# Expert tiles computed in pairs with turned operands, the state-space start spread over two tiles, and a 32-row expansion

## The reference

```python
x = x + xattn(layernorm(x), ctx, mask)      # 16 heads, softmax over 257 keys
x = x + ssm(layernorm(x))
x = x + ffn(layernorm(x))

def ssm(x):                                  # state-space part
    conv = causal_conv4(x @ W_in[:, :768])   # C, B, x for 16 heads
    dt = softplus(x @ W_in[:, 768:] + dt_bias); A = A_param * dt
    norm = exp(cumsum(A)) * cumsum(exp(-cumsum(A)))
    Y = ssd(xh, A, Bh, Ch)
    return (Y[0] / norm) @ W_out.T           # Y of batch 0 only, norm of every batch

def ffn(x):                                  # 8 experts, inner width 704
    gates = softmax of the 2 largest of x @ w_router.T
    for e in range(8):
        h = silu(x @ w_gate[e]) * (x @ w_up[e])
        out += gates[:, e:e+1] * (h @ w_down[e])
```

## Time and profile before

| | us |
|---|---|
| median of 3 runs (1501.18 to 1503.05) | 1502.03 |
| the profiled execution, its own time | 1488.71 |
| its span, first to last instruction | 1486.7 |
| TensorE busy in the span | 1410.8 (95%) |
| VectorE busy | 1124.9 (76%) |
| ScalarE busy | 996.1 (67%) |
| GpSimd busy | 833.8 (56%) |
| mean granted TensorE clock | 0.966 |

### The profile page before, as it was taken

The page is one execution under the profiler, slowest core; times in us unless marked ns, Lnnn a source line. Parts: engine busy times, 40 slices in busy tenths (PEclk is TensorE's granted clock), DMA queues, the critical chain, the costliest instruction groups (busy, mean ns, idle before and its releaser), DMA issues.

```text
span 1486.7 us, 53570 instructions
## 1 busy us (share of the span) xinstructions
PE 1410.8 (95%) x15668; PEld 1288.0 (87%) x15669; DVE 1124.9 (76%) x3999; ACT 996.1 (67%) x2482; POOL 833.8 (56%) x1401
## 2 busy tenths in 40 slices
PE   6969999999999999999999998579999999999997
PEld 5858888888888888888888887379999999999997
DVE  3647888888888888888888886468878777787775
ACT  4726777777777777777777775067777776777674
POOL 3514665665666656656656553236666665565554
PEclk9969999999999999999999998589999999999999
DMA  6212464454433433433433321435655555555554
GB/s 189 67 30 73 120 200 136 144 192 131 122 98 96 127 93 99 122 101 90 126 96 106 86 70 55 159 120 149 162 141 151 158 142 145 144 163 142 141 147 111
DMA packets 102009, 183.80 MB, mean 124 GB/s; under 512 B 19393, under 2 KB 61377, under 8 KB 101793
## 3 DMA queue, kind: packets, MB, share of 16 engines
q1 hardware_dynamic: 86272, 164.35, 36.5%
q0 software_dynamic: 15680, 18.76, 7.1%
HBM read 152.63 MB, written 31.13 MB: 124 GB/s over the span
## 4 chain that ended last, share of the span: by engine, by line
PE 84%; DMA 2%; issue 2%; POOL 2%; DVE 1%; ACT 1%; POOLq 1%; DVEq 0%; ACTq 0%; SPq 0%
PE k L412 16%; PE m L412 12%; PE v_p L412 11%; PE y_p L1478 9%; PE up_p L1478 9%; PE gate_p L1478 8%; PE sc L412 5%; PE pt L476 5%; PE v_p L476 4%; PE ht_p L1517 3%; PE m L496 2%; DMA par<-zbuf,gi 2%; PE z_p L1484 1%; POOL gi L1668 1%; POOLq L1667 0%
## 5 line engine op out<-in xcount | busy, mean ns | idle before, releaser
L738 ACT ACTIVATE wd<-wd,nmx 128x257 f32<-128x257 f32 x512 | 255.7, 503 | 31.0 <-DVE nmx L884 26.7
L714 ACT ACTIVATE wd<-v_p 128x512 f32<-128x512 f32 x256 | 152.6, 596 | 163.8 <-PE k L412 136.5
L1305 POOL TENSOR_TENSOR ctx_lo<-wd,ctx_hi 128x516 fp32r<-128x516 f32 x128 | 167.0, 1304 | 130.5 <-ACT ctx_hi L714 130.5
L884 DVE CUSTOM_DVE_ANT_0 wd<-sc,wd 128x257 f32<-128x257 f32 x512 | 191.4, 421 | 63.6 <-PE sc L412 57.3
L1680 POOL DMA_INDIRECT out<-par,oi x71 | 113.5, 1599 | 146.5 <-ACT par L1586 145.9
L412 PE MATMUL k<-ctx_hi,wkh 128*128 128x256 f32 x512 | 159.3, 311 | 1.7 <-POOL ctx_lo L1305 1.4
L1557 ACT ACTIVATE uw_hi<-wu 128x1408 fp32r x71 | 98.3, 1385 | 85.1 <-PE up_p L1478 84.8
L1668 POOL COPY oi<-par 128x4 int32 x71 | 148.1, 2087 | 0.0
L1615 DVE TENSOR_TENSOR uw_lo<-wu,uw_hi 128x1408 fp32r<-128x1408 f32 x71 | 115.4, 1625 | 41.3 <-ACT uw_hi L1557 41.3
L412 PE MATMUL k<-ctx_lo,wkh 128*128 128x256 f32 x512 | 145.3, 284 | 0.0
L1615 DVE TENSOR_TENSOR gw_lo<-wg,gw_hi 128x1408 fp32r<-128x1408 f32 x71 | 115.4, 1625 | 39.2 <-ACT gw_hi L1557 39.2
(11 more groups left out here) (200 smaller groups left out, 4678.8 us busy)
## 6 DMA issues: line engine op xcount, KB each, us to landing
dl<-d_low SPq DMA_DIRECT2D x71, 768.0 KB, 4.4
wd<-in_ctx SPq DMA_DIRECT2D x128, 258.0 KB, 2.7
wd<-in_mask SPq DMA_DIRECT2D x512, 32.1 KB, 1.8
wd<-in_wd SPq DMA_DIRECT2D x24, 256.0 KB
d_high<-wd SPq DMA_DIRECT2D x24, 256.0 KB
d_low<-wd SPq DMA_DIRECT2D x24, 256.0 KB
wd<-d_high SPq DMA_DIRECT2D x8, 768.0 KB, 9.2
wg<-in_wg SPq DMA_DIRECT2D x8, 704.0 KB
```

The lines of the kernel that those rows point to most:

```text
L714: return nc.scalar.activation(out, in_, ACT.Copy, **kw)
L738: nc.scalar.activation(pr[:, g, :], sm[:, g, :], ACT.Exp, bias=nmx[:, g:g + 1], scale=-1.0, accum_out=rsum[:, g:g + 1]).then_inc(exp_done, 1)
L884: V.tensor_tensor_reduce(sm[:, g, :], SC[g][:, 0:S], msk[:, b, :], -1.0, 3.0e38, ALU.add, ALU.min, nmx[:, g:g + 1]).then_inc(max_done, 1)
L1305: G.tensor_tensor(ctx_lo[:, b % 2], ctx[:, b], ctx_hi[:, b % 2].bitcast(F32), ALU.subtract).then_inc(lo_done, 1)
```

## The change

**First stage.** `expand` becomes four products of 32 rows each: `px` is laid out with 128 columns so that `RP` has the four groups of `rp` on four groups of 32 partitions, and each of the four products takes one group of rows and writes one of the four score banks `SC[r]` in place of a quarter of `M`. It now waits for `max_done` of the second batch of the tile, and `scores` at b = 2 waits for `t_done` (the wait in `turn_b` is gone). VectorE does `weigh` and `attention_out` before `statistics1`. The state-space part is cut up: TensorE projects (`ssd_project`) one step earlier, at the end of tile 1; VectorE's convolution (`ssd_conv`) closes step (1, 3); the running sums use the bank `pt` at the end of tile 1, with ScalarE's exponential in step (2, 0); and the rest (`ssd_mix`) stays in step (2, 0). `w4` is gone: 64 products of a 32x32 operand take the place of 16.

**Second stage.** The plan (25 operations in place of 10, 4 products in place of 2) now gives 28 pairs of tiles of one expert (`NPAIR`) and 15 single tiles (`NSLOT`). Singles run as before. For a pair the operands are turned: the weights are stationary and the 256 tokens move, so the product is h transposed and `turn_h` is not needed. The 704 inner columns are five chunks of 128 and one of 64; in the last chunk gate and up stand side by side in one product, its high and low parts of h are stacked in one operand, and a DRAM copy (`twin_out`) doubles the rows of the down weights to match. Weights are split once per pair, in one buffer, in pieces that follow TensorE's chunks.

```diff
 def expand(j):
     pe.wait_ge(rp_done, 4 * (j + 1))
-    for k, e in enumerate(("er", "ep")):
-        for a in range(NH):
-            o = (k * NH + a) * P
-            last = mm(M[:, o:o + P], cst(e)[:, a * P:(a + 1) * P], rp[:, :])
+    if runs(j + 1):
+        pe.wait_ge(max_done, 4 * (4 * (j + 1) + 2))
+    for r in range(NG):
+        rows = slice(r * Q, (r + 1) * Q)
+        last = mm(SC[r][:, 0:P], spread[rows, :], rp[rows, :])
     last.then_inc(ex_ready, 1)
...
+                if b == 2 and runs(i - 1):
+                    pe.wait_ge(t_done, 2 * i)
...
-            def ssd():
+            def ssd_project():
                 pe.wait_ge(wxbc_in, 16)
-                pe.wait_ge(a_done, 1)
-                pe.wait_ge(norm_done, 1)
+                pe.wait_ge(dt_done, 1)
...
+            def ssd_mix():
+                pe.wait_ge(norm_done, 1)
+                pe.wait_ge(ssd_dve, SSD_C)
...
                 for h in range(H):
-                    last = mm(M[:, h * HD:(h + 1) * HD], w4[:, h, :, :].rearrange("p b l -> p (b l)"),
-                              xs[:, h * HD:(h + 1) * HD])
+                    for b in range(TB):
+                        last = mm(M[b * Q:(b + 1) * Q, h * HD:(h + 1) * HD], ws[:, h, :], xs[:, h * HD:(h + 1) * HD])
```

The first two lines of the second piece are in `scores`. Then the order of work in a pair, of TensorE, POOL and ScalarE in turn:

```diff
+            def chunk(p, s, k):
+                if k == 0:
+                    pe.wait_ge(z_done, p + 1)
+                    pe.wait_ge(a_low, SPLIT_A * (p + 1))
+                if k == 2:
+                    pe.wait_ge(b_low, SPLIT_B * p + 2)
+                if k == FULL:
+                    pe.wait_ge(b_low, SPLIT_B * (p + 1))
+                at_least(pe, hf_done, FC * p + k - 2)
+                (zh, zl), (wh, wl) = zT2[s], w2
+                for side in range(1 if k == FULL else 2):
+                    o = 2 * k * P + side * P
+                    for c in range(NH):
+                        for j, (w, z) in enumerate(((wh, zh), (wh, zl), (wl, zh))):
+                            last = mm(G2[k % 3][:, side * F2:(side + 1) * F2], w[:, c, o:o + P], z[:, c, :],
+                                      c == 0 and j == 0, c == NH - 1 and j == 2)
+            def down_pair(p, s):
+                pe.wait_ge(h_low, FC * (p + 1))
+                for h in range(2):
+                    at_least(pe, yp_done, 2 * p + h - 1)
+                    for c in range(FC):
+                        terms = ((hh, wh), (hh, wl), (hl, wh))[:2 if c == FULL else 3]
...
+            def body2(p, s):
+                chunk(p, s, 0)
+                chunk(p, s, 1)
+                if not (isinstance(p, int) and p == 0):
+                    down_pair(p - 1, 1 - s)
...
+                    turn_pair(p + 1, 1 - s)
+                for k in range(2, FC):
+                    chunk(p, s, k)
...
+            def scatter_pair(p, s):
+                for h in range(2):
+                    held(pool, (tab_in, 16), (oi_done, p + 1), (yp_done, 2 * p + h + 1), (y_out, 16 * (2 * p + h)))
+                    G.indirect_dma_start(outd[:, :], bass.IndirectOffsetOnAxis(oi[:, s, h, 1:2].bitcast(U32), 0),
+                                         yb2[:, h, :], None, compute_op=ALU.add).then_inc(y_out, 16)
+            def body2(p, s):
+                if not (isinstance(p, int) and p >= NPAIR - 2):
+                    gather_pair(p + 2, s)
...
+                    pair_owners(oi[:, 1 - s], p - 1, oi_done)
+                    scatter_pair(p - 1, 1 - s)
...
+            def early(p, s):
+                e = nc.scalar.value_load(pair_expert(p), min_val=0, max_val=E - 1)
+                high_b(p, e, 0)
+                silu2(p, 0)
+                high_b(p, e, 1)
+                high_h(p, s, 0)
+                silu2(p, 1)
+                high_short(p, e)
+                high_h(p, s, 1)
+                if not final(p):
+                    high_a(p + 1)
+            def body2(p, s):
+                if not (isinstance(p, int) and p == 0):
+                    take_y2(p - 1, 1 - s, 0)
+                    take_y2(p - 1, 1 - s, 1)
...
+                    high_z(p + 1, 1 - s)
+                for k in (2, 3):
+                    silu2(p, k)
+                    high_h(p, s, k)
+                silu2(p, 4)
+                silu2(p, FULL)
+                high_h(p, s, 4)
+                high_h(p, s, FULL)
+                if not final(p):
+                    early(p + 1, 1 - s)
```

More of the change, by code:

```diff
@@ L224, in attend @@
         K2 = K[:, 0:NH * LAST].rearrange("p (a t) -> p a t", a=NH)
-        SC = [ps(f"sc{r}") for r in range(NG)]
+        SCORES = own.enter_context(nc.psum_tensor("sc", [P, NG, 512], F32))
+        SC = [SCORES[:, r, :] for r in range(NG)]
         PT = ps("pt")
@@ L1215, in tile @@
                         attention_out(i - 1)
+                    if b == 0 and runs(i + 2):
+                        statistics1(i + 2)
                     if b == 1 and runs(i - 1):
@@ L1409, in experts @@
[L1409 to L1415 removed]
+        F2 = 2 * P
@@ new lines, in experts, with part, cut @@
+        FULL = FC - 1
+        GU = 2 * FULL * P + 2 * FL
+        SPLIT_A, SPLIT_B = 2, 4
+        ZW, HK, WW = 2 * NH * F2, 2 * (FC + 2) * F2, 2 * NH * GU
+        places = dict(w=WW, z0=ZW, z1=ZW, x=768, ht=HK, dl=FC * D)
+        begin, at = {}, 0
+        for name, n in places.items():
+            begin[name] = at
+            at += n
+        room = sb("room", [P, at], F32R)
+        def part(name, skip, n):
+            return room[:, begin[name] + skip:begin[name] + skip + n]
+        def cut(name, skip, *shapes):
+            out = []
+            for shape in shapes:
+                n = 1
+                for k in shape:
+                    n *= k
+                names = " ".join("abcd"[:len(shape)])
+                sizes = {"abcd"[k]: shape[k] for k in range(len(shape))}
+                out.append(part(name, skip, n).rearrange(f"p ({names}) -> p {names}", **sizes))
+                skip += n
+            return out
@@ L1441, in flat, with pairs @@
             return part.rearrange("p c n -> p (c n)")
+        def pairs(eng, body):
+            body(0, 0)
+            body(1, 1)
+            with eng.Fori(2, NPAIR - 2, 2) as p:
+                body(p, 0)
+                body(p + 1, 1)
+            body(NPAIR - 2, 0)
+            body(NPAIR - 1, 1)
         def tiles(eng, body):
@@ L1478, in mm, with turn_pair @@
                 return nc.tensor.matmul(out, lhsT, rhs, start=start, stop=stop)
+            def turn_pair(p, s):
+                pe.wait_ge(zg_in[s], 32 * (turn(p, s) + 1))
+                at_least(pe, z_done, p)
+                for a in range(NH):
+                    for h in range(2):
+                        o = a * F2 + h * P
+                        last = nc.tensor.transpose(Z2[:, o:o + P], zg2[:, s, h, a * P:(a + 1) * P], ident)
+                last.then_inc(z_ready, 1)
             def turn_z(t, s):
-                pe.wait_ge(zg_in[s], 16 * (t // 2 + 1) if isinstance(t, int) else 16 * ((t - s) // 2 + 1))
@@ L1541, in body @@
                     down(t - 1, 1 - s)
+            turn_pair(0, 0)
             pe.wait_ge(wd_in, 16 * E)
+            pairs(pe, body2)
+            down_pair(NPAIR - 1, 1)
+            pe.wait_ge(info_done, 2)
             pe.wait_ge(blank, 1)
@@ L1684, in body @@
                 if not first:
-                    owners(oi[:, 1 - s, :], t - 1, oi_done)
-                if not last:
+                    owners(oi1[:, 1 - s, :], t - 1, oi_done)
+                if not first and not last:
                     gather(t + 2, s)
```

572 lines of the change are left out of this document (402 added, 170 removed).

## The result

The changed kernel takes 1478.18 us (median of 4, 1474.04 to 1480.19), the kernel before 1502.38 beside it. The ratio is 0.983 (95% interval 0.982 to 0.985): 24 us less, where 70 were forecast. Its profiled execution took 1479.7 us, with a span of 1477.9. Faster was right; 1478 lies above the range of 1414 to 1466.

The account below looks back on a forecast made before the run. TensorE was taken as the bound, holding 84% of the chain that ended last. Second stage 40.7, expansion 14.4 and state space 14.6 sum to 69.7 us off 1502.0, called 1432; range 1414 to 1447, with rivals 1414 to 1466.

Parts of the forecast that it names:

- Second stage, TensorE: Second stage: a pair's 100 products and 4 transposes take 12.34 us, two tiles 13.74 before; 28 pairs save 39.3 us.
- Second stage, POOL: Second stage: POOL's ring of copies, scatters, landing and gathers takes 12.1 us a pair (11.1 to 13.9), hidden under 12.34.
- rival A: Second stage: POOL's ring bounds the pairs at 13.2 us, 26 pairs lose 0.9 each; 1455 us, chance 0.25.
- Second stage, ends: Second stage's first pair and change-over to singles cost 3.6 us; gather waits gone give 5; the longer plan costs nothing.
- Expansion, the product: First stage: the 8 expansion passes take 0.35 us instead of 0.89, saving 0.54 a tile, 17 over 32.
- Expansion, `RP`: First stage: loading 128 columns instead of 32 costs 0.18 against about 0.16, 4 a tile: -2.6 us (0 to -6).
- net 14.4: First stage: the expansion's saving less the wider RP load, 14.4 us (6 to 20), with new waits costing nothing.
- rival B: First stage gives little: row groups do not overlap, VectorE late at step 0, state space at half clock; 1452, chance 0.12.
- State space: First stage's state-space part: 29.8 us lost before, 15 after; 14.6 saved (8 to 19).
- The 20 that I set against it: Sign of a right forecast: TensorE's idle time between 80 and 110 us falls to about 8 from 20.
- The 13.3 us "which I carry over": Whole kernel: the median time stands 13.3 us above the profiled execution, and the forecast keeps that offset.

Follow-up runs that it names:

- e8: Kernel before with the second stage in pairs and, on POOL, both gathers moved between a pair's two scatters; 1470.0 us, ratio 0.977.
- e4: Kernel before with only the second stage in pairs and the longer plan; 1458.1 us, ratio 0.982.
- e1: Kernel before, no edit, run again for its profile; 1485.1 us, ratio 1.001.
- e14: Changed kernel with softmax sums in four 32-row products, POOL's gathers between a pair's scatters, and slot-table writes at step 2; 1434.8 us, ratio 0.965 to the kernel before.
- e2: Kernel before with only the 32-row expansion, including the wide px load and statistics1 behind weigh; 1503.1 us, ratio 1.013.
- e3: Kernel before with only the spread state-space part; 1473.2 us, ratio 0.993.
- e12: Kernel before without POOL's two indirect writes a tile into the slot table and their waits; 1492.7 us, ratio 0.993.

## Why the prediction was wrong, point by point

- **Second stage, TensorE: right, 0.1 too low.** 100 products took 12.03 us and four transposes 0.44, so 12.47 for the 12.34 of the sum: a pitch of 0.120, not 0.119, and a slower first product at each of two joints (the four transposes take 0.44 as forecast). 27 x 0.13 = 3.5 us. Apart from POOL the others did keep up, as e8 shows.
- **Second stage, POOL: the failed step of this stage.** "Against 12.34 that is just hidden." From one output copy to the earliest start of the next I reckoned 12.1; the second round above takes 11.75 (1077.31 to 1089.06, the end of the oi copy and 0.09), the first 12.9 (from the output copy at 1064.39 to the one at 1077.31). In the first the terms that were too small are the two gathers, 2.9 for 2.3, and the copy of gi, 0.91 behind the scatter's end for 0.6 (inside its bounds of 0.2 to 1.1), under a VectorE operation of 0.96 with both inputs in SBUF; the landing with what follows it was 0.2 too large. Why the gathers take longer in one round is open. The sum was hardly off; what failed is to hold one value of it against 12.34. The mean of both rounds is 12.3, near my value; but the long round shows in full and the short one gives nothing back, since TensorE takes 12.47 anyway, and some pairs in a row are long. So the pairs cost 12.85. This is rival A at 0.5 us a pair where it had 0.9. The Trainium skill, "SBUF — State Buffer", section "Who interferes with whom", had the rule for the copy's part, 0.7 of the 1.2 us between the rounds: the copy ends with VectorE's difference, within 0.03 us.
- **Second stage, ends: right in size.** e4's second stage is 28.5 us shorter than e1's (481.6 against 510.1). 28 pairs at 12.82 for 13.74 make 25.8 of it, which leaves +2.7 for the ends, where the sum had +1.4. The plan cost nothing, as said. The changed kernel's own first profile has 25.1 in place of 28.5; 4 us of that are the two slow single tiles described at e8.
- **Expansion, the product: right.** From its start to the next it takes 0.43 where 8 passes in `M` took 0.98: 0.55 saved for the 0.54 of the sum. It starts 0.09 later behind the last value product, so 0.46 is left. The row groups do overlap behind full-width products.
- **Expansion, `RP`: the failed step of this stage, and the largest.** "`RP` loads 128 columns where it loaded 32; two of its passes then cost ... 0.18 against about 0.16 now." I priced the wide product by one that stands among wide products. It stands behind 32-column ones and costs 0.09 itself and 0.11 in them (0.02 come back behind it): 0.18 a step for 0.02, -23 us for -2.6, and outside the bound of -6.
- **Expansion, "net 14.4": a term put at nothing without a reason.** Even with the wide load's price taken off, 3.5 of 14 us arrive. I looked for new waits in the two that the change writes down, and both cost nothing. The one that came was an old one, `norm_done` ahead of the output product, which had no wait worth a row in e1. The change puts `statistics1`, 0.62 us of VectorE, behind `weigh` and so ahead of the norm, and my sum has no term for it. The output product then starts 0.3 us later a tile in e14 and 0.15 in e2. VectorE with its 82% was late at step 0: that half of rival B was right, though it came from the order of its list.
- **State space: 14.6 forecast, 12.9 measured by tile 5 in e3** (163.5 us from the first softmax sums before, 150.6 after), 9.8 in the time; within the 8 to 19. In e3 TensorE stands idle 5.6 us from 80 to 110, in the changed kernel 7.1, near the 8 of the forecast. The 20 that I set against it was wrong: in these 30 us TensorE stands idle 10.9 in the kernel before (10.0 of waits in the lines of the earlier trace rows), and busy time at half clock I had counted as lost as well. The sum itself had a slip: 29.8 - 15 is 14.8. The rows of e3:

```profile
80.00:90.00 10.00, 7.98 (x96) 6.03 (x95) 8.66 (x26) 5.09 (x18) 1.99 (x2) 1.00 0.03 9
90.00:100.00 10.00, 6.38 (x161) 3.88 (x159) 4.49 (x14) 2.87 (x7) 1.07 (x5) 0.76 0.15 35
100.00:110.00 10.00, 10.00 (x107) 8.72 (x108) 6.40 (x27) 5.86 (x19) 3.57 (x9) 0.90 0.21 55
```

- **The 13.3 us "which I carry over"** were no constant. The profile of the kernel before came from a run without the stretches, its times from runs with them: the tile of 27.38 us on which the sum rests was 28.2 in the runs that it was held against. The changed kernel loses less to them (28.6 against the 28.0 of e2), perhaps because its norm is late anyway; no run tests that. It is about 0.2 us in 23 tiles, 5 of the 10 us between the sum of the parts (-14.4) and the result (-24); the rest lies within the intervals of the ratios, each some 3 us to either side.

In sum, by the parts alone: 35 us of the miss lie in the expansion, 16 in the pairs, 5 in the state space. That is 55; the changed kernel missed by 45, and the 10 between are those of the last point.

## What to carry to other kernels

Price a product by one that stands behind the same neighbours: behind products of 32 columns a stationary load of all 128 cost 0.2 us more than one of 32, and four loads of 32 cost 0.02 more. Where a loop on one engine alternates between a long and a short round, compare each round with the bound that hides it, not their mean. And when a change moves work within the list of the next busiest engine, follow every old wait on what stands behind that work: 0.62 us of VectorE ahead of the norm took some 10 of the 14 us that TensorE's shorter list was worth.

## What was not expected of the hardware

The same program took 1483 to 1486 us in three series and 1502 in two. The 19 us are stretches of mostly 1.1 to 1.6 us, in each of some 23 tiles (28.2 us for 27.4), in which no engine's semaphore moves while instructions already released go on. They begin at POOL's indirect writes to the slot table and need them (gone in e12). A profile without them and times with them, as in the forecast, are in effect of two different kernels: 13 us here.
